# Sorted expert tiles: relu rows kept transposed, closing normalisations beside the tiles, results added by index into the output

## The reference, cut to what matters

```python
x = x + layernorm(attn(layernorm(x)))        # 16 heads of 8 channels, 256 keys
x = x + layernorm(ffn(layernorm(x)))
# ffn: y = LN(u + mha(u)) * g1 + be1         # 4 heads, attention across the 16 batches
#      z = LN(y + moe(y)) * g2 + be2
# moe: idx = argmax(y @ Wg.T) over 8 experts, for each row on its own
#      out = relu(y @ W1[e] + b1[e]) @ W2[e] + b2[e]     for e = idx, 128 -> 512 -> 128
```

## Time and profile before

| | us |
|---|---|
| median of 3 runs | 764.3 (750.58 to 766.88) |
| the profiled execution | 755.61 |
| its span, first to last instruction | 753.8 |
| first layer, until its barrier | to about 379 |
| second attention, until its barrier | to about 577.7 |
| expert tiles | 578.6 to about 679 |
| closing part | 679.8 to 753.8 |

### The profile page before, as it was taken

One profiled execution on the slowest core, in us unless ns is written; L12 is line 12 of the kernel. 1 busy time (PEld: TensorE's weight loads), 2 busy tenths in 40 slices (PEclk: granted clock), 3 DMA queues, 4 the chain that ended last, 5 costly groups with the idle time before them and its releaser, 6 DMA issues. The chain is left out here.

```text
span 753.8 us, 16521 instructions
## 1 busy us (share of the span) xinstructions
PE 583.6 (77%) x5290; PEld 415.8 (55%) x5290; DVE 461.2 (61%) x1252; ACT 391.6 (52%) x990; POOL 294.6 (39%) x554
## 2 busy tenths in 40 slices
PE   4999999999999999999548888887411999980000
PEld 3665666666666666666337777776410777760000
DVE  2555666667666666664137888789551666653676
ACT  1025665656565656566228978786100566650435
POOL 5402233333333333112242577676871000007884
PEclk9559999999999999999759999997555999995555
DMA  5000000000000000000084000000111111111121
GB/s 148 6 1 3 2 3 10 10 9 10 10 9 10 10 10 10 10 10 9 19 257 141 1 3 2 0 0 15 40 49 52 54 56 56 56 38 42 59 65 57
DMA packets 27361, 25.43 MB, mean 34 GB/s; under 512 B 3864, under 2 KB 22048, under 8 KB 27296
## 3 DMA queue, kind: packets, MB, share of 16 engines
q1 hardware_dynamic: 19088, 17.58, 7.8%
q0 software_dynamic: 2048, 4.20, 1.8%
q10 hardware_dynamic: 6160, 2.82, 1.3%
HBM read 14.49 MB, written 7.73 MB: 29 GB/s over the span
## 5 line engine op out<-in xcount | busy, mean ns | idle before, releaser
L369 DVE TENSOR_REDUCE nmax<-psA 128x2 f32<-128x512 f32 x256 | 165.3, 688 | 120.7 <-PE psA L200 120.4
L497 ACT ACTIVATE pr<-psB 128x512 f32<-128x512 f32 x256 | 138.9, 595 | 127.9 <-PE psB L212 127.8
L200 PE MATMUL psA<-km,q 24*128 24x256 f32 x768 | 138.9, 425 | 3.8 <-POOL km L589 2.1
L212 PE MATMUL psB<-q,km 26*128 26x256 f32 (+1 forms) x768 | 113.7, 411 | 0.0
L200 PEld LDWEIGHTS psA<-km,q 24*128 24x128 f32 x768 | 91.3, 196 | 29.5 <-issue 17.6
L1559 POOL DMA_INDIRECT moe<-moe_sorted,back_i x32 | 32.8, 1024 | 110.5 <-DMA moe_sorted<-os 102.0
L212 PEld LDWEIGHTS psB<-q,km 26*128 26x128 f32 (+1 forms) x768 | 71.5, 189 | 1.4 <-issue 0.9
L589 POOL TENSOR_TENSOR km<-kraw,rows_of 128x768 f32<-128x768 f32 x16 | 23.5, 1466 | 118.6 <-DVEq L348 114.0
L226 PE MATMUL psO<-pr,v 128*32 128x256 f32 x1024 | 69.4, 389 | 0.0
L1432 DVE COPY own<-e_first 128x1152 f32 x39 | 29.6, 760 | 39.4 <-PE psH L1397 24.8
L563 POOL TENSOR_SCALAR ve<-mv_r 128x2 f32<-128x2 f32 x16 | 3.7, 231 | 127.4 <-DVE mv_r L330 127.4
(11 more groups left out here) (194 smaller groups left out, 1272.2 us busy)
## 6 DMA issues: line engine op xcount, KB each, us to landing
ys<-y_sorted SPq DMA_DIRECT2D x39, 64.0 KB, 1.7
moe_sorted<-os ACTq DMA_DIRECT2D x39, 64.0 KB, 1.6
xs<-x_all SPq DMA_DIRECT2D x16, 128.0 KB
e_first<-W SPq DMA_DIRECT2D x1, 2048.0 KB, 8.4
e_first<-b SPq DMA_DIRECT2D x1, 2048.0 KB, 19.5
out<-xs SPq DMA_DIRECT2D x8, 256.0 KB
x_all<-x SPq DMA_DIRECT2D x1, 1536.0 KB, 10.7
q<-mT SPq DMA_DIRECT2D x64, 4.0 KB
```

What stands on the lines that cost most here:

```text
L200: last = T.matmul(psA[:, n % 2, c * L1:(c + 1) * L1], queries(b, h, depth, slice(c * P, (c + 1) * P)), keys(b, h, depth, slice(0, L1)), st ...
L212: last = T.matmul(psB[:, (16 * b + h) % 3, c * L1:(c + 1) * L1], keys(b, h, depth, slice(c * P, (c + 1) * P)), queries(b, h, depth, slice( ...
L369: V.tensor_reduce(nmax[:, b % 2, :, h], psA[:, n % 2, :].rearrange("p (c m) -> p c m", c=2), AX.X, ALU.max, negate=True).then_inc(S["a_fre ...
L497: A.activation(pr[:, h % PRING, :, :].rearrange("p c l -> p (c l)"), psB[:, (16 * b + h) % 3, :], ACT.Exp, scale=SCALE1).then_inc(S["b_fre ...
```

## The change

The layout of the work in `experts` is new, and its two parts become one.

- **Tiles.** PE computes the hidden rows already transposed (four products of 128 columns, `own` as the stationary side), so the four transpositions (L1405) and ACT's copy of them go. DVE takes max(h, -b1) straight from PSUM; since relu(h + b1) = max(h, -b1) + b1, the missing b1 @ W2 is put into the second bias, which a fifth product (`top`, `b2p`) adds in PSUM. PE reads W2 in place, with an index that it loads itself. ACT fetches W1.
- **b1 @ W2** is computed once, in step 19 of the second attention (one transposition and 32 small products on PE, two copies on ACT, two additions on DVE).
- **Closing.** The normalisations are done on the sorted rows, in groups of `SIZES` = 4 (eight times), 3, 2, 2 tiles, between the tiles: the DVE, ACT and POOL steps of group g stand a fixed number of steps (2, 3, 4, 8, 9, 10, 11) behind the group's last tile.
- **Output.** The first layer also writes x1 to `out` (`x1_out`). Each finished tile `wz` is added to `out` with an indirect DMA that adds to what stands there (`put`, 39 of them on POOL). The row numbers travel with the rows: a sorted row now has 144 numbers instead of 128, the 129th being its place in `out`. Rows of padding get places of their own behind the real output. `moe_sorted`, the gathers and the final store go.
- **Rings.** SP loads tiles into `ys`, a ring of 16, and since a `put` reads its places from there, the load of tile t waits until the `put` of tile t-16 has landed. `wz` is a ring of 8.
- **Weights.** b1 and b2 are no longer spread over 128 partitions by DMA.
- **First layer, last batch.** Scores are issued four heads at a time, into five PSUM banks.
- The loops over tiles are written out in full on each engine.

```diff
+        def bank_of(b, h):
+
+            if b < LAST:
+                return psB[:, (16 * b + h) % 3, :]
+            return psB[:, h % 5, :] if h % 5 < 3 else psA[:, h % 5 - 3, :]
...
-                    if here:
+                    if here and next_:
                         scores(i, 2 * g)
                         scores(i, 2 * g + 1)
+                    if here and not next_ and g % 2 == 0:
+                        for h in range(2 * g, 2 * g + 4):
+                            scores(i, h)
...
+            def x1_out(b):
+
+                sp.dma_start(out[b * L1:(b + 1) * L1, :].rearrange("(p c) d -> p c d", p=P),
+                             x_all[:, 2 * b:2 * b + 2, :]).then_inc(kept, 16)
...
+            x1_out(LAST)
             sp.wait_ge(S["stored"], 16 * B1)
+            sp.wait_ge(kept, 16 * B1)
...
+YROW = P + 16
+NPAD = NE + NS - NT
 CHUNK = 8
 SORT_AT = {16: 0, 17: 1, 20: 2}
+BIAS_AT = 19
...
+                if isinstance(t, int) and t == BIAS_AT:
+                    pe.wait_ge(loaded, 16 * len(loads))
+                    pe.wait_ge(S["p_ok"], 8 * NSTEP)
+                    T.transpose(psS[0][:, 0:NE * DF // P], w["b1n"][:, :], ident[0:NE * DF // P, 0:NE * DF // P]
+                                ).then_inc(S["b1_full"], 1)
+                    pe.wait_ge(S["biases"], 2)
+                    for e in range(NE):
+                        to = psS[e // 4][0:1, (e % 4) * P:(e % 4 + 1) * P]
+                        for f in range(DF // P):
+                            last = T.matmul(to, w["b1T"][:, e * 4 + f:e * 4 + f + 1], w["w2"][:, f, e * P:(e + 1) * P],
+                                            start=(f == 0), stop=(f == DF // P - 1))
+                    last.then_inc(S["b2_full"], 1)
...
-            G.memset(zeros[:, :], 0.0).then_inc(S["zeros_ok"], 1)
+            G.memset(zeros[:, :, :], 0.0).then_inc(S["ids_ok"], 1)
+            pool.wait_ge(S["ids_ok"], 1)
+            G.iota(zeros[:, :, P:P + 1].bitcast(I32), [[1, NPAD]], base=B1 * L1, channel_multiplier=NPAD
+                   ).then_inc(S["zeros_ok"], 1)
+            G.memset(y_all[:, :, P:], 0.0)
+            G.memset(w["b2p"][:, :], 0.0)
+            G.memset(w["top"][:, :], 0.0).then_inc(S["ids_ok"], 1)
+            pool.wait_ge(S["ids_ok"], 2)
+            G.memset(w["top"][0:1, :], 1.0).then_inc(S["ids_ok"], 1)
+            G.iota(y_all[:, :, P:P + 1].bitcast(I32), [[1, NT]], base=0, channel_multiplier=NT
+                   ).then_inc(S["ids_ok"], 1)
+            pool.wait_ge(S["ids_ok"], 4)
...
+RING = 16
+WRING = 8
+SIZES = [4] * 8 + [3, 2, 2]
+FIRST = [sum(SIZES[:g]) for g in range(len(SIZES))]
+GROUPS = len(SIZES)
...
+        def at(t, lag):
+
+            for g in range(GROUPS):
+                if t == ends(g) - 1 + lag:
+                    return g
+            return None
+
+        def members(t, lag):
+
+            turns = [(g, t - (ends(g) - 1 + lag)) for g in range(GROUPS)]
+            return [(g, k) for g, k in turns if 0 <= k < SIZES[g]]
...
+            def turn(t):
+                pe.wait_ge(S[f"ys{t % RING}"], 16 * (t // RING + 1))
+                if t >= 2:
+                    pe.wait_ge(S["yT_ok"], t - 1)
+                T.transpose(psT[t % 2][:, 0:P], ys[:, t % RING, 0:P], ident[:, :]).then_inc(S["t_full"], 1)
...
+            def hidden(t):
+                pe.wait_ge(S["yT_ok"], t + 1)
+                pe.wait_ge(S["own_ok"], t + 1)
+                if t >= 2:
+                    pe.wait_ge(S["h_ok"], t - 1)
+                for f in range(NF):
+                    last = T.matmul(psH[t % 2][:, f * P:(f + 1) * P], own[:, t % 3, f * P:(f + 1) * P],
+                                    yT[:, t % 3, :], start=True, stop=True)
+                last.then_inc(S["h_full"], 1)
...
+            def output(t):
+                g = group(t)
+                k = t - FIRST[g]
+                e = pe.value_load(w2_i[0:1, t:t + 1], min_val=0, max_val=(NE - 1) * P)
+                pe.wait_ge(S["h_ok"], t + 1)
+                if k == 0 and g >= 2:
+                    pe.wait_ge(S["z0_ok"], g - 1)
+                to = psO[g % 2][:, k * P:(k + 1) * P]
+                T.matmul(to, w["top"][:, :], w["b2p"][:, bass.ds(e, P)], start=True, stop=False)
+                for f in range(NF):
+                    last = T.matmul(to, hT[:, t % 2, f, :], w["w2"][:, f, bass.ds(e, P)], start=False,
+                                    stop=(f == NF - 1))
+                last.then_inc(S["o_full"], 1)
+
+            turn(0)
+            turn(1)
+            for t in range(NS + 1):
+                if t < NS:
+                    hidden(t)
+                if t + 2 < NS:
+                    turn(t + 2)
+                if t >= 1:
+                    output(t - 1)
...
+                V.tensor_tensor(hT[:, t % 2, :, :], psH[t % 2][:, :].rearrange("p (f n) -> p f n", f=NF),
+                                w["nb1T"][:, bass.ds(e, NF)].unsqueeze(2).broadcast_to([P, NF, P]),
+                                ALU.max).then_inc(S["h_ok"], 1)
...
+            for t in range(STEPS):
+                if t < NS:
+                    relu(t)
+                if (g := at(t, 2)) is not None:
+                    summed(g)
+                    statistics(0, g, range(0, min(2, SIZES[g])), z0[:, g % 2, :, :])
+                if (g := at(t, 3)) is not None:
+                    if SIZES[g] > 2:
+                        statistics(0, g, range(2, SIZES[g]), z0[:, g % 2, :, :])
+                    moments(0, g)
+                if (g := at(t, 8)) is not None:
+                    affine(g)
+                if (g := at(t, 9)) is not None:
+                    statistics(1, g, range(SIZES[g]), z2[:, g % 2, :, :])
+                    moments(1, g)
...
+            def fetch(t):
+                e = act.value_load(w1_i[0:1, t:t + 1], min_val=0, max_val=(NE - 1) * DF)
+                if t >= 3:
+                    act.wait_ge(S["h_full"], t - 2)
+                A.activation(own[:, t % 3, :], w["w1"][:, bass.ds(e, DF)], ACT.Copy).then_inc(S["own_ok"], 1)
...
+                A.activation(yT[:, t % 3, :], psT[t % 2][:, 0:P], ACT.Copy).then_inc(S["yT_ok"], 1)
...
+            for t in range(STEPS):
+                if t + 2 < NS:
+                    fetch(t + 2)
+                    turned(t + 2)
+                for g, k in members(t, 4):
+                    act.wait_ge(S["rs0"], g + 1)
+                    if g >= 2:
+                        act.wait_ge(S["z2_step"], g - 1)
+                    apply(0, g, k, z1[:, g % 2, k, :], z0[:, g % 2, k, :]).then_inc(S["z1_ok"], 1)
+                for g, k in members(t, 10):
+                    n = FIRST[g] + k
+                    act.wait_ge(S["rs1"], g + 1)
+                    if n >= WRING:
+                        act.wait_ge(S[f"put{n % WRING}"], 16 * (n // WRING))
+                    apply(1, g, k, wz[:, n % WRING, :], z2[:, g % 2, k, :]).then_inc(S["w_ok"], 1)
...
+            def put(t):
+                pool.wait_ge(S["w_ok"], t + 1)
+                G.indirect_dma_start(out, bass.IndirectOffsetOnAxis(ids[:, t % RING, P:P + 1], 0),
+                                     wz[:, t % WRING, :], None, compute_op=ALU.add
+                                     ).then_inc(S[f"put{t % WRING}"], 16)
+
+            pool.wait_ge(kept, 16 * B1)
+            for t in range(STEPS):
+                if (g := at(t, 3)) is not None:
+                    scale(0, g)
+                if (g := at(t, 9)) is not None:
+                    scale(1, g)
+                for g, k in members(t, 11):
+                    put(FIRST[g] + k)
...
+            for t in range(NS):
+                r = sp.value_load(row_i[0:1, t:t + 1], min_val=0, max_val=LAST_ROW - P)
+                if t >= RING:
+                    before = t - RING
+                    sp.wait_ge(S[f"put{before % WRING}"], 16 * (before // WRING + 1))
+                sp.dma_start(ys[:, t % RING, :], y_sorted[bass.ds(r, P), :]).then_inc(S[f"ys{t % RING}"], 16)
```

More of the change, by code:

```diff
@@ L1077, in iteration @@
                     find(SORT_AT[t])
+                if isinstance(t, int) and t == BIAS_AT + 1:
+                    dve.wait_ge(S["b2_full"], 1)
+                    dve.wait_ge(S["ids_ok"], 3)
+                    for k in range(2):
+                        V.tensor_tensor(w["b2p"][0:1, k * 512:(k + 1) * 512], psS[k][0:1, :],
+                                        w["b2r"][0:1, k * 512:(k + 1) * 512], ALU.add).then_inc(S["biases"], 1)
             pipeline(iteration)(dve)
@@ new lines, in experts @@
+        ve = [sb(f"ve_z{k}", [P, 2, 4]) for k in range(2)]
+        rs = [sb(f"rs_z{k}", [P, 2, 4]) for k in range(2)]
+        nb = [sb(f"nb_z{k}", [P, 2, 4]) for k in range(2)]
+        half4 = sb("half4", [P, 4])
+        psT, psH, psO = pb("psT"), pb("psH"), pb("psO")
+        names = ["consts", "t_full", "yT_ok", "own_ok", "h_full", "h_ok", "o_full", "z0_ok", "st0", "st1", "mv0",
```

(4 more changed lines are left out.)

384 lines of the change are left out of this document (124 added, 260 removed).

## The result

Before the change 757.9 us (median of 4 runs, 750.6 to 766.9), after it 897.9 us (4 runs, 894.2 to 901.1): ratio 1.195, interval 1.188 to 1.202. The forecast was 918 us, its range 873 to 965. The profiled execution took 901.1 us, its span is 899.1.

The account below looks back on a forecast made before the run. A ring of latencies, one turn per tile, was to bound the expert block: 577.7 us to its barrier, +8 for edits ahead, 330 for the block, 0.5 last wait, 1.8 beyond the span, giving 918 us; range 873 to 965.

Parts of the forecast that it names:

- the ring: Expert block, tiles 16 to 38: load of n+16 waits for put n, whose `wz` follows copy n+15; 7.35 us a turn.
- the two kinds of turns: Ring: short turns of 7.35 us alternate with long ones of mean 13.8, whose put stands behind a scaling awaiting DVE's statistics.
- Rival 3: Expert block: `wz` of tile n does not need the copy of tile n+15; tiles run at 2.1 to 2.3, 712 us; chance 0.05.
- rival 2: Ring: the adding DMA lands far later, say 6 us, adding 79 us: about 1,000 us; chance 0.08.
- rival 1: Ring: PE keeps the full clock, long steps lose about 2.3 us, short ones 0.3: 880 us; chance 0.07.
- One sign of the forecast: Expert block: granted PE clock falls to 0.5 about 40 us into the block and stays there.
- fill, to tile 15: Expert block, barrier to tile 15's transposition: 38 us, made of 4.6, 13.4, 19.0 and 0.9, plus 3 for index reads.
- tiles 17 to 38: Ring in the expert block: 11 short steps of 7.35 and 11 long ones of 14.0, 235 us.
- the tail: End of expert block: 7.5 us to the first of 16 puts, 31.6 on POOL with 8 scalings, landing 2.4: 41.5 us.
- The adding put: Ring and tail: put's issue on POOL with its hand-over 1.3 us, its landing 2.4 us.
- The edits ahead: Ahead of the expert block: memsets +4, b1 @ W2 +5, x1_out +0.5, four heads at a time -1.5; sum +8 us.
- the b1 @ W2 block: Ahead of the last batch's projection: 64 PE passes, 14 us at slow clock or 7 at full; +5, between 0 and 8.

Follow-up runs that it names:

- the scores alone: Kernel before with only the last batch's scores four heads at a time over five banks: 748.5 us (10 runs), ratio 0.996.
- the kernel with the wide tile of zeros: Kernel before with its eight padding writes read from eight different stretches of a wider zero tile: 751.1 us, one run.

## Why the prediction was right, and which terms were off

**The mechanism held: the ring, its links, and the two kinds of turns.** Loads wait for puts (229 us, 23 times); the ring opens with four more slots (721 us with 20, 714 with 24), for the most part with the closing steps drawn together (762 us), and a little with ACT's order turned (861 us); the long turns vanish when the puts go ahead of the scalings (818 us). No engine was the bound. Rival 3 (`wz` does not need the copy) is out by the timeline above, rival 2 (landing at 6 us) by 3.3 us from issue to landing, and rival 1 by a clock of 0.55 to 0.62. One sign of the forecast was off: the clock did not stay at 0.50, it rose to about 1.00 for short stretches. In three of the eleven long turns only 3.6 to 3.8 us passed from ACT's copy to DVE's maximum, where the slow clock takes 4.7; the forecast had priced them all at 1.2 GHz.

The forecast of 918 lies 17 us above the profiled execution (901.1) and 20 above the median. 9 of the 17 lie in the block, 8 ahead of it; in both parts larger errors went against each other, so that the total came out this close is luck in part.

**The block, from its barrier to the span's end: 321 us measured, 330 forecast.** By the copies of the transposed tiles:

- fill, to tile 15: copy at 611.29, 33.3 us behind the barrier at 577.98; forecast 41. The clock rose earlier than in the earlier trace rows: tiles follow each other at 1.9 and 1.7 us from the third, and at 2.12 from the fifth (forecast 2.11). This is the largest error of the block. 3 us of it are index reads that cost nothing there: PE never stood idle for one in the first sixteen tiles. In the turns behind, 23 of them (0.30 us each) left it idle for 7.8 us in all.
- tile 16: 12.2 us (12.3)
- tiles 17 to 38: 228.7 us (235). Eleven short turns of 6.9 to 7.2 us, mean 7.03 (7.35), eleven long ones of 13.1 to 15.0, mean 13.75 (14.0). The terms of the forecast's short turn add up to 7.31 and not 7.35, which is worth less than 0.5 us over the eleven.
- the tail: 46.9 us (41.5). 16 puts as forecast, the first 7.6 us behind the last copy, but 35.8 us for them instead of 31.6. With its hand-over a put took 1.9 us and not 1.3, 9 us more for 16; about 5 of these came back, since six scalings stood among the puts, at 0.9 to 1.4 us each, and not eight at 1.35. Then 3.5 for the landing and the last wait.

**The adding put.** I took 1.3 us with its hand-over and 2.4 for the landing, 3.7 together. It is 1.58 + 0.16 and 1.79 to SP's next load, 3.5. The two errors nearly cancel in the ring, and the first shows in the tail. The Trainium skill (DMA: Bandwidth & Descriptors, section on the anatomy of one DMA on the SWDGE path) gives 2.15 us for 64 KB by its formula (an estimate), and its fixed part holds setup and completion handling. The prediction set this against the time behind the issue (and reckoned 911 us from it, where 24 landings at 0.25 us less give 912); from the start of the issue to the landing this case shows 2.3 us without the addition, near the page's figure, and 3.3 with it. The same section calls the generation of descriptors a small, variable part; here the whole issue, of which it is one part, holds POOL for 0.96 us in a plain send of 128 rows and for 1.58 in an adding one.

**The edits ahead, forecast +8, came out at about -1 where the clock stays up.** The barrier stands at 572.0 with 24 slots (570.7 to 572.1 in six profiles). In the kernel before it would stand at 572.9 if the sends ended the block there too, 2.94 us behind the last of them, and in the kernel with the wide tile of zeros it stands at 573.3; with the scores alone at 567.7. The pieces:

- four heads at a time: -1.5 was too little. Two single profiles show 573.3 - 567.7 = 5.6 us, 4.0 of them at the last `x_all`; the timed runs 3.1 us (0.4% of 751, interval 0.8 to 5.4)
- memsets and index fills: +4 forecast, 3.3 measured (from the first memset to POOL's first work on the statistics 7.15 us, 381.60 to 388.75, against 3.84 in the earlier trace rows)
- x1_out: 5.6 us from the last `x_all` to the barrier's other side with it, 5.4 without; 0.2, forecast 0.5
- the b1 @ W2 block: +5 forecast, nothing measured. It took PE 8.7 us, at a mean clock of 0.81 (0.50 in the six us ahead of it; 7 us were reckoned for the full clock, 14 for the slow one), and what it cost was below what single profiles resolve (six of them differ by 1.4 us at the barrier): 572.0 - 567.7 = 4.3 us hold memsets (3.3), x1_out (0.2) and this
- the padding writes: "end the block as before" failed. It was true of one execution only.

In the profiled execution after, the clock's fall in the last batch (+6.0 at the barrier, 578.0 against 572.0) and the missing slow row (-4.9) nearly cancelled, so its experts began where they did before. The forecast's +8 and the measured 0 look like one error of 8 us; they are four.

PE's index read: I took 0.2 us a long turn; idle for it PE stood 0.34 us a turn. The Trainium skill (DMA: Bandwidth & Descriptors, section on latency and other measured facts) puts a floor of about 600 ns under such loads. The profile after shows 0.30 us on PE and 0.27 on SP, about half of it: the measurement decides.

## What to carry to other kernels

When a slot is given back by the last step of a long pipeline, don't compare the ring's size with the lag of that step alone. Write down, for the instruction that frees the slot, what stands ahead of it in the list of each engine on its way; the lookahead of the front eats slots too. If only one slot is to spare, the kernel runs at one tile per round trip, whatever the engines could do. Four more slots gave it all back here (721 us), closing steps drawn together on three engines most of it (762), the order on one engine alone a fifth (861).

A second habit: take a row that a term leans on from more than one execution if you can. A slow stretch on a queue and a dip of the clock moved 5 and 6 us here, more than any of the edits ahead that I costed.

## What the runs showed of the hardware

- An indirect write of 128 rows of 512 bytes that adds to DRAM holds POOL 1.55 to 1.58 us (0.96 to 1.03 where it only writes), with 0.30 between two puts and 0.16 behind a scaling, and lands 3.3 us after its issue begins (2.3).
- POOL's power of 128x4 takes 1.04 us alone; beside 90% of puts and a busy DVE the group of all 22 (16 of them 128x4) averages 1.43 us with 24 slots, 1.13 with 16.
- A square root on ACT (0.20 us for 128x4) and DVE's reciprocal (0.17) take the place of POOL's 1.04; the table for the root cost one load of 1.28 us.
- The same 18 products of PE took 4.21 us at a granted clock of 0.50 and 2.27 at 1.00.
- Unchanged instructions got a granted clock of 1.00 or 0.57 over 345 to 357 us in different executions of one kernel.
- SP issued eight writes in 16.4 us in one execution and, unchanged, in 8.14 and 8.16 in two others.
